# Who makes five low parts early in a split-precision product: GpSimd or VectorE

## What is computed

```python
# layer 0: a dense product, and a gated low-rank one (8 experts of rank 16)
base   = einsum('btd,od->bto', x, W)
logits = einsum('btd,ed->bte', x, Wr) + 5.0 * one_hot(language_ids, 8)[:, None, :]
topw, topi = top_k(logits, 2)
gates  = sum(one_hot(topi, 8) * softmax(topw)[..., None], axis=-2)
h      = einsum('btd,erd->bter', x, A)
x = x + base + 2.0 * einsum('bter,bte,eor->bto', h, gates, B)
# layer 1: each row has its own 1024 x 1024 matrix, chosen among 16
x = x + einsum('bsi,boi->bso', x, weight[adapter_ids])
```

## Time and profile before

| | us |
|---|---|
| median of 3 runs | 396.98 (396.69 to 397.53) |
| profiled execution, its own time | 396.9 |
| span of that execution | 395.1 |
| TensorE busy | 389.8 |
| VectorE busy | 307.9 |
| ScalarE busy | 173.8 |
| GpSimd busy | 60.7 |

### The profile page before, as it was taken

How to read it: one execution, slowest core, us unless ns; L and a number is a source line. 1 busy time by engine, 2 the same in 40 slices (tenths; PEclk the granted TensorE clock), 3 DMA queues, 4 the chain that set the end, 5 groups by cost and what they waited for, 6 DMA issues and landing times.

```text
span 395.1 us, 5948 instructions
## 1 busy us (share of the span) xinstructions
PE 389.8 (99%) x1888; PEld 329.9 (83%) x1888; DVE 307.9 (78%) x415; ACT 173.8 (44%) x245; POOL 60.7 (15%) x86
## 2 busy tenths in 40 slices
PE   8999999999999999999999999999999999999996
PEld 8888988888889888888888888888888888888886
DVE  3899998988554757048877967999999999999600
ACT  3362283554400243254275334555665656556411
POOL 3134300000000000000110211332321231312000
PEclk9999999999999999999999999999999999999999
DMA  7999750113776100009492999999999999897212
GB/s 202 226 224 216 109 147 2 53 55 107 234 217 165 25 1 0 2 1 247 130 330 71 274 265 273 274 253 278 259 280 291 286 267 302 256 268 166 80 53 55
DMA packets 88129, 68.60 MB, mean 174 GB/s; under 512 B 16386, under 2 KB 87074, under 8 KB 87586
## 3 DMA queue, kind: packets, MB, share of 16 engines
q1 hardware_dynamic: 61472, 46.59, 49.2%
q10 hardware_dynamic: 26626, 21.64, 17.9%
HBM read 53.51 MB, written 14.68 MB: 173 GB/s over the span
## 4 chain that ended last, share of the span: by engine, by line
PE 97%; DMA 1%; SPq 1%; issue 0%; DVE 0%; ACT 0%
PE banks L1421 15%; PE banks L1419 15%; PE banks L1420 15%; PE banks L1282 13%; PE banks L1284 13%; PE banks L1283 13%; PE banks L1275 6%; PE banks L1260 2%; PE banks L1296 2%; PE banks L1293 2%; PE banks L1295 2%; DMA sums<-in_L_cond_Wr_dram 1%; PE banks L1314 0%; SPq L436 0%; SPq L483 0%; SPq L429 0%
## 5 line engine op out<-in xcount | busy, mean ns | idle before, releaser
L1282 PE MATMUL banks<-ring,weights 128*128 128x512 f32 x192 | 75.2, 392 | 0.0
L1420 PE MATMUL banks<-weights,tokens 128*128 128x512 f32 (+1 forms) x184 | 69.9, 380 | 0.0
L1421 PE MATMUL banks<-weights,tokens 128*128 128x512 f32 (+1 forms) x184 | 69.9, 380 | 0.0
L1419 PE MATMUL banks<-weights,tokens 128*128 128x512 f32 (+1 forms) x184 | 69.9, 380 | 0.0
L1106 ACT ACTIVATE weights<-weights_f 128x1024 fp32r<-128x1024 f32 x44 | 46.6, 1061 | 50.1 <-DVE weights_f L759 49.3
L512 POOL TENSOR_TENSOR raw<-raw,ident 128x128 f32<-128x128 f32 x42 | 30.0, 714 | 219.2 <-DMA raw<-in_L_cond_weight_dram 219.1
L759 DVE STREAM_TRANSPOSE weights_f<-raw 128x1024 f32<-128x1024 f32 x42 | 51.7, 1232 | 8.2 <-POOL raw L512 7.7
L765 DVE TENSOR_TENSOR weights<-weights_f,weights 128x1024 fp32r<-128x1024 f32 x44 | 52.7, 1198 | 0.7 <-ACT weights L1106 0.6
L1284 PE MATMUL banks<-ring,turned_w 128*128 128x512 f32 x128 | 49.8, 389 | 0.0
L1283 PE MATMUL banks<-tokens,weights 128*128 128x512 f32 x128 | 49.8, 389 | 0.0
L1282 PEld LDWEIGHTS banks<-ring,weights 128*128 128x128 f32 x192 | 36.0, 188 | 7.6 <-issue 0.3
(11 more groups left out here) (131 smaller groups left out, 626.0 us busy)
## 6 DMA issues: line engine op xcount, KB each, us to landing
raw<-in_L_cond_weight_dram SPq DMA_DIRECT2D x168, 128.0 KB, 5.2
ring_f<-in_L_cond_weight_dram SPq DMA_DIRECT2D x88, 128.0 KB, 5.5
out_dram<-sums ACTq DMA_DIRECT2D x31, 256.0 KB, 5.6
raw<-in_x_dram SPq DMA_DIRECT2D x48, 128.0 KB, 3.3
x_kept<-stage ACTq DMA_DIRECT2D x24, 256.0 KB, 3.1
raw<-in_L_cond_W_dram SPq DMA_DIRECT2D x16, 128.0 KB, 3.4
turned_w_f<-in_x_dram SPq DMA_DIRECT2D x12, 128.0 KB, 3.4
ring_f<-in_L_cond_W_dram SPq DMA_DIRECT2D x12, 128.0 KB, 3.6
```

What stands on the lines that cost most here:

```text
L1282: nc.tensor.matmul(ps, u_hi, x_hi, start=first and k == 0, stop=False, skip_group_check=True)
L1419: nc.tensor.matmul(ps, x_hi, w_hi, start=m == 0, stop=False)
L1420: nc.tensor.matmul(ps, x_hi, w_lo, start=False, stop=False)
L1421: mm = nc.tensor.matmul(ps, x_lo, w_hi, start=False, stop=m == M - 1)
```

## The change

The five lows of GpSimd (`xl` 1 and 2, `wr` 1 to 3) are made by VectorE, each at a place between its turns. GpSimd's own `low`, its semaphore and its waits go. `LOW_AT` becomes the place in the whole list, and that list has a new order: wl1, wl2, wr1, wl3, wr2, wr3 in place of wl1, wr1, wl2, wr2, wl3, wr3. ScalarE makes its high parts in the new order. TensorE's wait ahead of product 1 is for the low of `xl` 3, and its second wait ahead of product 2 falls away.

```diff
--- before.py
+++ after.py
@@ -94,9 +94,8 @@
             BEFORE[item] = here[k - 1] if k else None
 
 
-
     PIECES = [("xl", t) for t in range(XT)] + [("wl", 0)]
-    PIECES += [(kind, r) for r in range(1, HM) for kind in ("wl", "wr")]
+    PIECES += [("wl", 1), ("wl", 2), ("wr", 1), ("wl", 3), ("wr", 2), ("wr", 3)]
     PIECES += [("xr", t) for t in range(XT)] + [("wr", 0)]
     PIECES += [("x", 0, 6, t) for t in range(XT)] + [("u", 6, r) for r in range(HM)]
     PIECES += [("u", 7, r) for r in range(HM)] + [("x", 0, 7, k) for k in range(HM)] + [("b",)]
@@ -107,8 +106,7 @@
     for i in ORDER:
         PIECES += [("x", 1, i, k) for k in range(HM)]
     PIECE_AT = {p: k for k, p in enumerate(PIECES)}
-    POOL_PIECES = [("xl", 1), ("xl", 2), ("wr", 1), ("wr", 2), ("wr", 3)]
-    LOW_AT = {p: k for k, p in enumerate(p for p in PIECES if p not in POOL_PIECES)}
+    LOW_AT = PIECE_AT
 
 
 
@@ -303,7 +301,6 @@
         w_loaded = [sem(f"w{r}_loaded") for r in range(HM)]
         a_loaded = [sem(f"a{'lr'[h]}_loaded") for h in range(2)]
         diagonal = sem("diagonal")
-        pool_lo_done = sem("pool_lo_done")
         wr_loaded = sem("wr_loaded")
         lang_loaded = sem("lang_loaded")
         adapters_loaded = sem("adapters_loaded")
@@ -532,21 +529,8 @@
                 a11, a21 = quarter_w(7, r), quarter_w(5, r)
                 nc.gpsimd.tensor_tensor(a11, a11, a21, ALU.subtract).then_inc(s3_done, 1)
 
-            def low(p):
-                pool.wait_ge(hi_done, PIECE_AT[p] + 1)
-                src, high_part, low_part = sides(p)
-                nc.gpsimd.tensor_tensor(low_part, src, high_part.bitcast(F32), ALU.subtract).then_inc(pool_lo_done, 1)
-
-
-
-            low(("xl", 1))
-            low(("xl", 2))
-            pool.wait_ge(diagonal, 3)
-            low(("wr", 1))
-            pool.wait_ge(lo_done, LOW_AT["wl", 3] + 1)
-            low(("wr", 2))
-            pool.wait_ge(lo_done, LOW_AT["xr", 1] + 1)
-            low(("wr", 3))
+
+
             pool.wait_ge(lang_loaded, 16)
             nc.gpsimd.tensor_copy(lang_f[:], lang_i[:]).then_inc(setup, 1)
             for t in range(XT):
@@ -773,9 +757,11 @@
             turn_half(("ah", 0))
             dve.wait_ge(wr_loaded, Q * 16)
             nc.vector.transpose(fac[:, :, ER:ER + S], wr_raw.rearrange("p (m j) -> p m j", m=M)).then_inc(fac_done, 1)
+            low(("xl", 1))
             turn_half(("wh", 0, 0))
             dve.wait_ge(consts, 3)
             add_diagonal(0)
+            low(("xl", 2))
             low(("xl", 3))
             low(("wl", 0))
             turn(("w", 1))
@@ -786,8 +772,11 @@
             turn(("w", 3))
             low(("wl", 2))
             add_diagonal(3)
+            low(("wr", 1))
+            low(("wl", 3))
             turn_half(("ah", 1))
-            low(("wl", 3))
+            low(("wr", 2))
+            low(("wr", 3))
             turn_half(("xh", 0, 1))
             turn_half(("xh", 1, 1))
             low(("xr", 0))
@@ -1131,9 +1120,11 @@
                 high(("xl", t))
             high(("wl", 0))
             act.dma_start(lang_i[:], lang_ids.partition_broadcast(P)).then_inc(lang_loaded, 16)
-            for r in range(1, HM):
+            high(("wl", 1))
+            for r in range(2, HM):
                 high(("wl", r))
-                high(("wr", r))
+                high(("wr", r - 1))
+            high(("wr", HM - 1))
             copy_p1(0, 0)
             copy_p1(0, 1)
             high(("xr", 0))
@@ -1322,14 +1313,13 @@
 
             def first_products():
                 first_features(0)
-                pe.wait_ge(pool_lo_done, 2)
+                pe.wait_ge(lo_done, LOW_AT["xl", 3] + 1)
                 for r in range(HM):
                     pe.wait_ge(lo_done, LOW_AT["wl", r] + 1)
                     for k in range(HM):
                         step(0, 1, k, r, main_bank(0, r), True)
                 first_features(1)
                 pe.wait_ge(lo_done, LOW_AT["wr", 0] + 1)
-                pe.wait_ge(pool_lo_done, len(POOL_PIECES))
                 for r in range(HM):
                     if r == DRAINED:
                         pe.wait_ge(h_copied, 1)
```

## The result

The kernel after takes 397.79 us (median of 13 runs, 397.31 to 398.72), the kernel before beside it 397.20 us (13 runs, 396.69 to 397.56). The ratio is 1.0018, 95% interval 1.0011 to 1.0026: slower by 0.6 to 0.7 us, where 1.6 was forecast. Two executions far off the rest, at a mean granted clock of 0.66 and 0.76, are in no ratio (565.74 us of the kernel before, 493.29 us of one experiment).

A forecast was written before the change was run, and what follows sets the result against it. TensorE, never dry after 10.55 us, was taken to bound the kernel. wr0 2.0 us late less 0.37 slack gives 1.63, with wl1's 0.44 in it: 396.98 + 1.63 = 398.6 us, range 397.9 to 399.4.

The forecast's parts named there:

- What bounds the kernel: Whole span: TensorE never runs dry after 10.55 us, so any later wait of it is added whole.
- The slot: Each low added to VectorE costs 0.61 us from start to start; five make 3.05 us.
- xl1 for nothing: Ahead of the turn of w0's left half, xl1's 0.61 us fits in a 0.67 us load wait: cost 0.
- wl1: Product 1's wait for wl1's low: no slack before, so TensorE stalls 0.44 us, load at 17.37 instead of 16.93.
- wr0 late by 2.0 us on VectorE: Ahead of product 2: 3.05 - 0.61 - 0.17 - 0.19 - 0.08 = 2.0 us late, making TensorE 1.63 us late.
- wl2's 0.84: wl2's low on VectorE, lengthened beside GpSimd's low, returns to 0.65; 0.19 us comes back.
- the slack at wr0: At product 2's first load, wr0's low is ready 0.37 us early before the change, which reduces the delay.
- The term for late loads that take up part of the delay: VectorE's timeline marks no load wait between 11.16 and 30.87, so late loads swallow nothing of the delay.
- The first: Rival at wr0: not slower, VectorE regains what GpSimd took, or late loads swallow the delay; 397.4 us, chance 0.08.
- Rival 2: Delay grows: ScalarE waits return in full, xl1 isn't hidden, or product 7's slack fails; 399.1 to 399.5 us, chance 0.10.
- Rival 3: The 1.2 us hole at wr0 costs TensorE its clock, 2.7 us more, 401.3 us; chance 0.04.
- the prediction's own signs of being wrong: wr0's low begins before 28.9, TensorE waits again after 31, or the features start elsewhere than 10.5.

The follow-up runs named there:

- both halves: Two kernels from before: only xl1 and xl2 to VectorE, 396.86 us, ratio 0.9998; only wr1, wr2 and wr3 to VectorE, 397.50 us, ratio 1.0017.
- the second of after: The kernel after, unchanged, run again for a second profile: 398.15 us.
- the two extra lows: The kernel after with two more lows of the same size on VectorE beside those of wr2 and wr3: 400.07 us, ratio 1.0071 to before.
- the second profile of before: The kernel before, unchanged, run again for a second profile: 396.94 us.
- x's two lows: From the kernel before, only xl1 and xl2 go to VectorE; wr1 to wr3 stay with GpSimd: 396.86 us, ratio 0.9998.
- before with the swap: The kernel before with wr0's low ahead of the turn of the first x tile of the right token blocks: 397.38 us, ratio 1.0006.
- the second (0.29%): The kernel after, unchanged, timed again beside the other experiments on one chip: 397.92 us (7 runs), ratio 1.0029 to before.

## Why the prediction was right or wrong

- **What bounds the kernel: right for TensorE, incomplete for VectorE.** The span is the moment of product 2's first load plus 366.2 to 366.3 us, in the profiles of before and after and of both halves (366.5 in the second of after, with one more hole of 0.3 us in layer 1). But "VectorE's list against TensorE's" left out what VectorE itself is held by.
- **The slot, and xl1 for nothing: right.** 0.61 us by the two extra lows (1.22 for two). In the first profile of after xl1 stands between the turn of Wr at 9.00 and that of w0's left half at 10.14, whose distance had been 1.11 us without it.
- **wl1: right.** Forecast 0.44 us, seen 0.45 to 0.57 in the eight profiles with xl2 on VectorE.
- **wr0 late by 2.0 us on VectorE: right.** 1.94 by two profiles of after. wl2's 0.84 became 0.65, as written.
- **The step that failed: the slack at wr0, 28.86 - 28.49 = 0.37 us.** It was read from one execution in which w0's left half had been turned 0.1 to 1.2 us later than in the others (at 11.16; from 10.00 to 11.07 elsewhere, in some of them behind xl1's low). There VectorE had no wait for x's right halves. In the second profile of before it waits 0.96 us for them and TensorE waits 0.63 us for wr0: the slack isn't +0.37 but -0.63, and 0.96 of the 1.94 us fall into idle time. Then the change costs 1.94 - 0.96 = 1.0 us. Between executions that both start late it is 1.5. Where w0's left half is turned sooner still, more falls into idle time. An estimate from rows: VectorE's list of before takes 20.52 - 11.16 = 9.36 us from that turn to x's right halves. With the turn at 10.21 and x's halves at 20.84, as with x's two lows, that leaves 1.27 us idle and a cost of 0.7; with 10.00 and 20.45, as in before with the swap, 1.09 idle and 0.85. The ratios gave 0.6 to 0.7 and 1.1 us, near the lower end and the middle of these; how many executions have which landings isn't known. The term for late loads that take up part of the delay was mis-sized: 0 written, up to 0.96 measured. The range had the same gap: the 0.61 us of xl1 were "to be kept for the range", but its upper end still takes them off, and its lower end has no term for a wait on x's loads.
- **The rivals.** The first had two parts. Its GpSimd part fell: 0.19 us came back, no more. Its second part, late loads that swallow the delay, I dismissed with "marks no wait for a load between 11.16 and 30.87", a true sentence on one execution. That is what happened, with half of the delay. Rival 2 didn't come: nothing is lost at product 7 in three profiles of the kernel after. Rival 3 didn't come at the change's hole (0.94 us by TensorE's own record, granted clock 1.00); a fall like it stands behind one of 2.14 us.
- **The number.** 398.6 was forecast and 397.79 measured, just outside the low end of 397.9; as a difference to the before of its own comparison, +0.6 where +1.6 was forecast. The direction was right. Two of the prediction's own signs of being wrong showed in the first profile of after: the features started at 9.50, not near 10.5, and wr0's low began at 28.73, before 28.9, though not because VectorE was quicker than its slots. By the bound of 0.2% the first comparison (0.18%) is on the edge of "no change" and the second (0.29%) beyond it.

## What to carry to other kernels

A slack that is read from one profile holds for the landings of that execution. Before a move onto a full engine is priced, take a second profile of the kernel before and look for waits on loads that the first doesn't show: an engine without idle time in one execution may have 1 us of it in the next. And count how much fits ahead of a landing: here three of five moved operations cost nothing that could be measured, and two more than the five cost their full slot.

## What the runs showed of the hardware

- VectorE beside GpSimd. From the kernel with x's two lows moved, VectorE and then GpSimd:

```profile
16.45 1.24 DVE L593 STREAM_TRANSPOSE turned_w_f<-ring_f 128x1024 f32<-128x1024 f32 x1
17.61 0.86 DVE L610 TENSOR_TENSOR weights<-turned_w_f,weights 128x512 fp32r<-128x512 f32 x1
```

```profile
16.62 1.30 POOL L538 TENSOR_TENSOR weights<-turned_w_f,weights 128x512 fp32r<-128x512 f32 x1 [14.73 <-DVE turned_w_f L599]
```

  The turn at 16.45, which runs beside GpSimd nearly all the time, takes its usual 1.24 us. The low that begins at 17.61, 0.31 us before GpSimd ends at 17.92, takes 0.86 instead of 0.65. The product by a constant above, begun 0.09 us behind the start of GpSimd's low, took 1.25 instead of 0.18 and was over 0.05 us behind its end. They were lengthened by 0.21 of the 0.31 us that GpSimd still had, and by 1.07 of 1.20. So these two wait for GpSimd's end for all but some 0.1 us, and turns don't. Nor does an addition with one operand in PSUM: `sums<-banks,sums` at 34.97 in the first profile of before, begun 0.39 us before GpSimd ends, takes its usual 0.65. This agrees with what the Trainium skill says on the page "SBUF — State Buffer", section "SBUF: two separate sides": a GpSimd operation and a VectorE operation with two inputs in SBUF, or in a mode that uses both ports, exclude one another for a whole instruction. Which mode the product by a constant ran in, no run shows. It was worth only 0.19 us in the change, because most of the time that GpSimd's lows took in the kernel before lay beside turns.
- TensorE's granted clock was 0.50 for some 3 us behind one hole of 2.1 us in a stream of matmuls, and that cost 1.6 us; behind holes of 0.9, 1.4 and 1.6 us it stayed at 1.00. It is one profile; by their mean clock of 0.996 two of four executions of that kernel had such a fall.
- The first loads land at varying moments. In before, a wait for w0's left half ended at 11.16 in one execution and at 10.56 in the other, and at 10.00 in before with the swap, whose program is the same up to there: 1.2 us in all. SyncE issues its first loads at 0.75 us in each of the first two profiles of before and of after.
